# A graph network's edge pass: the second-layer matmuls of a batch in one block of sixteen instead of four blocks of four

## The reference

```python
out = h = relu(x @ lin0_w.T + lin0_b)
eh  = relu(e_feat @ en1_w.T + en1_b)                  # 200,000 x 128, once
w_e = (eh @ en2_w.T + en2_b).reshape(-1, 32, 32)      # a 32x32 matrix for each edge
for _ in range(6):
    msg = einsum('ei,eio->eo', out[src], w_e)         # each edge's message
    agg = segment_sum(msg, dst, num_segments=6250) + conv_bias
    h   = gru_cell(relu(agg), h)
    out = h
```

## Time and profile before

| | before |
|---|---|
| median of 3 runs | 34,976.55 us (34,972.99 to 34,978.08) |
| the profiled execution | 34,982.19 us, its span in the trace 34,980.4 us |
| TensorE busy with matmuls | 20,562.4 us (59%) |
| ScalarE busy | 10,358.5 us (30%) |
| VectorE busy | 10,599.1 us (30%) |
| GpSimd busy | 22,641.0 us (65%) |
| mean granted TensorE clock | 0.78 of full speed |

### The profile page before, as it was taken

How to read it: one execution, slowest core, us unless ns; L and a number is a source line. 1 busy time by engine, 2 the same in 40 slices (tenths; PEclk the granted TensorE clock), 3 DMA queues, 4 the chain that set the end, 5 groups by cost and what they waited for, 6 DMA issues and landing times. The chain is left out here.

```text
span 34980.4 us, 467404 instructions
## 1 busy us (share of the span) xinstructions
PE 20562.4 (59%) x139128; PEld 8821.7 (25%) x139128; DVE 10599.1 (30%) x15910; ACT 10358.5 (30%) x27640; POOL 22641.0 (65%) x23430
## 2 busy tenths in 40 slices
PE   5557110110110799899999989989998996111111
PEld 3333100100100233333333333333333332000000
DVE  7665000000000344344444434434443442000000
ACT  0004100000000355455445545545554553000000
POOL 6880676677677566566556656647665664775775
PEclk8779555555555899999999999999999998555555
DMA  2115114113112322522522242252243224114014
GB/s 64 23 23 190 21 15 14 19 15 14 19 15 14 51 61 61 51 61 61 53 59 60 60 52 60 61 51 62 61 59 54 60 61 40 15 15 17 15 15 17
DMA packets 2058079, 1520.36 MB, mean 43 GB/s; under 512 B 1419487, under 2 KB 1801927, under 8 KB 2054464
## 3 DMA queue, kind: packets, MB, share of 16 engines
q0 software_dynamic: 749568, 390.42, 16.8%
q1 hardware_dynamic: 878380, 953.21, 9.1%
q10 hardware_dynamic: 430032, 175.29, 1.9%
HBM read 1250.48 MB, written 253.52 MB: 43 GB/s over the span
## 5 line engine op out<-in xcount | busy, mean ns | idle before, releaser
L613 POOL DMA_INDIRECT sb_xs<-node_rows,sb_idx x21824 | 20655.1, 946 | 11479.6 <-issue 6504.6
L713 PE MATMUL banks<-sb_spread,sb_eh_sb 128*128 128x512 f32 x23808 | 11923.9, 624 | 202.9 <-DVE sb_spread L668 169.5
L668 DVE TENSOR_TENSOR sb_spread<-sb_xs,banks_p 128x2048 f32<-128x2048 f32 x2976 | 6793.5, 2287 | 9479.0 <-PE banks L713 8282.7
L778 ACT ACTIVATE sb_g<-banks 128x512 f32<-128x512 f32 x11904 | 6962.7, 596 | 6043.9 <-PE banks L713 6008.2
L693 PE MATMUL banks_s<-sb_mask,sb_xs 128*32 128x16 f32 x43648 | 990.7, 202 | 10714.5 <-DMA sb_xs<-node_rows,sb_idx 10714.0
L772 ACT ACTIVATE sb_s<-banks_s 32x32 f32<-32x32 f32 x10912 | 2048.3, 188 | 12201.0 <-PE banks_s L693 11924.7
L713 PEld LDWEIGHTS banks<-sb_spread,sb_eh_sb 128*128 128x128 f32 x23808 | 4072.3, 190 | 5020.9 <-issue 4325.7
L650 DVE TENSOR_TENSOR sb_mask<-sb_meta_t,sb_node 128x128 f32<-128x128 f32 x2728 | 789.9, 290 | 11950.7 <-PE banks_s L693 11862.4
L701 PE MATMUL banks_p<-sb_g,sb_en 128*32 128x256 f32 x47616 | 3814.4, 393 | 3.9 <-ACT sb_pj L787 3.9
L693 PEld LDWEIGHTS banks_s<-sb_mask,sb_xs 128*32 128x32 f32 x43648 | 719.1, 128 | 10955.4 <-issue 10333.5
L271 POOL DMA_INDIRECT slots<-sb_rows,sb_slot_u x1600 | 1985.1, 1241 | 700.4 <-issue 696.8
(11 more groups left out here) (183 smaller groups left out, 8703.3 us busy)
## 6 DMA issues: line engine op xcount, KB each, us to landing
sb_eh_sb<-eh SPq DMA_DIRECT2D x1488, 512.0 KB
sb_xs<-node_rows,sb_idx POOLq DMA_INDIRECT x21824, 2.3
eh<-sb_eh_sb ACTq DMA_DIRECT2D x248, 512.0 KB, 3.2
sb_idx<-sb_src_t SPq DMA_DIRECT2D x2728, 4.0 KB, 1.7
parts<-sb_part ACTq DMA_DIRECT2D x2728, 16.0 KB, 1.4
sb_g<-parts SPq DMA_DIRECT2D x44, 992.0 KB
slots<-sb_zeros SPq DMA_DIRECT2D x16, 2294.0 KB, 45.8
sb_rowin<-slots SPq DMA_DIRECT2D x248, 148.0 KB, 3.3
```

The costliest lines, as they stand in the source:

```text
L613: nc.gpsimd.indirect_dma_start(m.xs[h][:, t * D:(t + 1) * D], None, m.node_dram, bass.IndirectOffsetOnAxis(ap=m.idx[h][:, t:t + 1], axis=0 ...
L668: V.tensor_tensor(m.spread[q], m.xs[h].rearrange("s (t i) -> s t i", i=D)[:, tiles, :].unsqueeze(3) .broadcast_to([P, TS, D, WN]), m.mask_ ...
L713: mm(m.ps_g[:, t % 4, :], m.eh[h][:, t * K:(t + 1) * K], m.spread[t // TS][:, t % TS, :, :], start=True, stop=True).then_inc(g_done, 1)
L778: nc.scalar.activation(m.g[h // 2][:, :, (h % 2) * TC + t, :], m.ps_g[:, t % 4, :].rearrange("k (i n) -> k i n", n=WN), copy).then_inc(g_s ...
```

## The change

`group` is called at another place in `outer`. Before, four of the sixteen matmuls of a batch stood behind its second, fourth, sixth and eighth outer product. Now all sixteen stand behind the fourth (`TS` is 4). The waits that the first group of a pair needs move with it, and so does the signal `grouped` of the last.

```diff
-                    if t == 1 and h % 2 == 0:
+                    if t == TS - 1 and h % 2 == 0:
                         pe.wait_ge(g_sb, n * TC + 4)
                         pe.wait_ge(pj_sb, n + 2)
-                    if t % 2 == 1:
-                        first = (h % 2) * D // 2 + 2 * (t - 1)
-                        last = group(range(first, first + 4), 1 - h // 2)
-                    if t == TC - 1 and h % 2 == 1:
-                        last.then_inc(grouped, 2)
+                    if t == TS - 1:
+                        first = (h % 2) * D // 2
+                        last = group(range(first, first + D // 2), 1 - h // 2)
+                        if h % 2 == 1:
+                            last.then_inc(grouped, 2)
```

## The result

The changed kernel took 34,077.24 us (median of 4 runs, 34,071.62 to 34,083.43) against 34,974.94 us of the kernel before on the same chip: ratio 0.9743, 95% interval 0.9726 to 0.9760, a gain of 898 us. A later repetition gave 34,082.60 us and 0.9742 (0.9726 to 0.9758).

The account below looks back on a forecast made before the run. TensorE was taken to bound a pass until DMA does at its end; fewer changes between matmul kinds save 1.13 us a pair, 645 pairs make 729 us, so 34,976.6 becomes 34,250 us, with a range of 34,140 to 34,420.

Parts of the forecast that it names:

- What bounds the kernel: Inside a pass: a long part bound by TensorE, then from about 20,054 us a short one bound by DMA at 0.93.
- The rival by which they gain too: Passes' ends: if TensorE's latency counted there too, 93 more pairs gain 105 us, giving 34,143 us; chance 0.07.
- What a round is made of: TensorE's four rounds a batch, 2.48 us each: 0.20 us lost around outer products, 0.14 around a group, 0.34 a round trip.
- the two ends for leaving towards `fold`: Second run of four outer products: 3.62 us if leaving for `fold` costs what a group does, 3.53 if nothing.
- How often: Batches before DMA fills up: 215 a pass gain, 107.5 pairs; six passes make 645 pairs x 1.13 = 729 us.
- the odd batch's wait: Before `fold`, behind ScalarE's eighth copy and `pj` copy: 1.27 us uncovered, odd batch 10.37 us against 10.63, gain 0.26.
- 1.13 taken: Gain of a pair of batches in us, taken from 1.09 to 1.18: even batch 0.83 to 0.92, odd 0.26.
- That switching isn't the cost: TensorE's rounds: the 0.34 us stays whatever the order, lost cover adds 368 us, giving 35,345 us; chance 0.05.
- that the gathers' loop holds the pace: Indices, gathers and landing, not TensorE, set 11.1 us a batch: 34,976 us, or about 34,910; chance 0.05.
- that a part is given back to GpSimd: GpSimd's 0.5 us margin: uneven steps or landing cost 0.2 to 0.4 us a batch, giving 34,510 to 34,770; chance 0.10.

Follow-up runs that it names:

- the early copy: Changed kernel with ScalarE's copy into `pj` behind the fourth copy into `g`, not the eighth: 33,664.75 us, 0.9623 of the kernel before; 0.9624 to 0.9714 on chips with stalls.

## Why the prediction was wrong in its size

**What bounds the kernel** held. Mid-pass TensorE did, the ends of the passes are bound by DMA as before and gained next to nothing: fold 210 to fold 247 of a pass took 442.9 us before and 440.8 after. The rival by which they gain too would give a time near the measured one, 34,143, for a reason that the trace excludes.

**What a round is made of** held to 0.01 us. The run of four was predicted at 3.62 and took 3.63, the block 1.86 and took 1.87. Of the two ends for leaving towards `fold`, 3.62 and 3.53, the trace gives 3.54. So the change between kinds does cost 0.34 us, 0.20 around the outer products and 0.14 around the group, and saving six of eight changes a batch is where the gain comes from. The kernels with other numbers of changes bear this out in their stall-free pairs: two blocks of eight 20.84 us and one block at the end 20.17, both within 0.03 us of what these prices gave with the wait read as below, against 22.18 for four groups. That a load overlaps a running matmul of the same rows is seen once more, in `fold`'s load at 24002.80, against the rule of the Trainium skill ("TensorE: Matmul & The Clock Gate", What overlaps and what doesn't).

**How often** held: 645 pairs x 1.42 = 916 us, against 905.65 between the two profiled executions. Up to fold 210 a pass got shorter by 148.8 us, not by the 121 (107.5 x 1.13) of the forecast.

**The step that failed** is the odd batch's wait: "the eighth copy starts at 25016.55, the `pj` copy at 25017.20, and `fold` at 25017.71, which is 1.27 us after the run's end. Now no group lies in these 1.27 us." The 0.65 us between the two copies was read as ScalarE's own time. It was the last group: the copy waits for `grouped` and starts 0.495 us after that group's last record does. With the signal early, the copy follows the eighth one after 0.494 us, and `fold` stands 1.629 us after the last outer record's start, not 1.790: 0.16 us a pair. The idle time ahead of every second `fold` is 1.04 us, where some 1.2 was forecast. Three experiments bear the reading out. The kernel that moves only the groups' places by one shows the same 0.494 and 1.63 us, with all the changes between kinds kept, and a stall-free pair of 22.79 us (22.8 by this reading, 23.07 by the prediction's). Two blocks of eight give 20.84 (20.87 and 20.44). And with the early copy the `pj` copy again starts 0.495 us after the block's last record, though the copy into `g` ahead of it started 1.94 us earlier. So the group cost the odd batch something of its own, beside covering part of the wait.

**A term that was missing**: `fold`'s first weight load. The sum took the 0.81 us of `fold` and `sum_rows` as given, but behind an outer product the load hides where `fold` doesn't wait, 0.458 instead of 0.557 us to `sum_rows`, 0.10 us a pair. The kernel with the early copy shows it in both batches, as both folds follow a run there.

The ledger of a pair, in us: 1.13 taken, + 0.04 (the low end for leaving towards `fold`), + 0.15 (4.74 instead of 4.89 from the second run's start to the waiting `fold`), + 0.10 (the load) = 1.42, as measured. Times 645 the three are 187 us, more than the 169 us between 898 and 729. The range was too narrow below for one reason: it had the unknown of the first term only, and none for a time between two records that was taken over unexamined.

**The rivals.** That switching isn't the cost, that the gathers' loop holds the pace, and that a part is given back to GpSimd: none of them happened on the first chip. The last is what bounds the kernel with the early copy. On a chip with stalls the result was near "no difference" (0.9985) for a reason that no rival named.

**What stays open.** What causes the stalls on chips 15, 10 and 5. It isn't these kernels' order, as the same program runs with and without them. It isn't the length of the block as such: the block of 32 matmuls at a pass's end (64 records) takes 3.28 us from its first record's start to its last's in every pass of every run, with stalls or without. The bursts of the `eh` loads alone don't explain them, as they appear in the propagation passes too, which load no `eh` (between 7000 and 8000 us a batch takes 11.6 us there, 10.0 on the first chip). An obvious suspect, TensorE's instructions coming in late by DMA, doesn't show either: both kernels have 99 packets in the queues marked "instruction" on either kind of chip, and none between 24000 and 25000 us. What does go with the stalls are the gathers: where GpSimd has issued its last of a pass, the stalls end (most other transfers are over there too, the share of DMA is 0.04). No run took the gathers away on such a chip, and no record says what else ran on those chips, so this is where a next experiment would start. Open too is what the block behind the eighth outer product gives with the gathers running and without stalls, and why DMA-bound ends of passes got longer with the early copy.

## What to carry to other kernels

Where two kinds of matmul take turns, read the rate of each from a long run and from a short one: the difference is the price of changing, and gathering the small kind into one block saves it as often as changes go. Before taking over a gap between two records, ask which of two releasers ended it; a copy behind another copy may have waited for something else that is over at nearly the same time. A constant gap doesn't tell, as both gaps were constant here to 0.002 us; moving one of the two releasers does. Where stalls blur a run, look for the batches that have none: they repeat to 0.01 us, and their length settles what the medians can't. And once the block stands in the middle, move what the block releases to right behind it: the copy into `pj` behind the fourth copy gave a further 1.2% here, and then eight gathers of 1.25 us set the pace.

## What the runs showed of the hardware that was not expected

- The same kernel took 34,975 and 34,982 us in two sets of runs and 40,757 to 41,655 us in four others, on three chips. On the slower ones TensorE's records keep their pace at the full clock (eight outer records in 3.70 us), but stalls stand between them (up to 2.8 us inside a block of the changed kernel), other engines go on up to 6 us after the TensorE record that they wait for, and the granted clock from 18500 to 19000 us, mid-pass, is 0.85 to 0.98 instead of 1.00. A ratio of kernels holds for the kind of chip that it was measured on: 0.974 and 0.9985 for one and the same change.
- On the slower chips the stalls of a pass end with its gathers, in all fourteen runs: two stretches behind them repeat to 0.01 us and for both kernels equal the shortest pair mid-pass on the first chip (22.18 and 20.78 us).
- A ScalarE copy of 256 columns starts 0.494 us after the start of a copy of 512 columns whose own record lasts 0.60 us.
- A weight load of `fold` (128x128) runs under an outer product that uses the same rows, and hides 0.10 us.
